# Attention written out without its loop, outputs accumulated in a PSUM bank, tables read in place

## The chip, the core and the metric

The kernel runs on one core of a Trainium2 chip. The core has engines that run side by side and meet through semaphores: PE (matrix products, written into PSUM), DVE and ACT (vector and scalar work), POOL (vector work on SBUF alone), and SP, which here only issues DMAs. The metric is the time of one execution on the device, in microseconds (us).

## The reference

A residual stream x of 8 batches x 512 tokens x 128 channels passes four layers, each with a layer norm ahead: attention, experts, a state-space mixer, experts again. The change lies in attention alone. Cut to what matters:

```python
scores = einsum('bhid,bhjd->bhij', q, k) * SCALE          # 16 heads of 64, n = 512
dist = clip(coords[:, None] - coords[None, :], -64, 64) + 64
scores = scores + einsum('bhid,ijd->bhij', q, rel_k_emb[dist])
threshold = top_k(scores, 32)[0][..., -1:]
attn = softmax(where(scores < threshold, -inf, scores))
res, v_curr = 0, v
for i in range(3):
    a_v = einsum('bhij,bhjd->bhid', attn, v_curr)
    if i == 0: a_v = a_v + einsum('bhij,ijd->bhid', attn, rel_v_emb[dist])
    v_curr = a_v
    res = res + sigmoid(alphas_raw)[i] * v_curr
x = x + res @ Wout.T + bout
```

All of it is float32.

## The kernel before

Attention works on pairs of heads: 8 pairs for each of 8 batches, 64 iterations (`ITS`). An iteration has four slots, T = 0 to 3, one for each tile of 128 queries. The five engines each run the same list of slots with their own `body`; each step of a slot works on a tile some slots back (`z.back(n)`), so that the stages of a tile are spread over eight slots: product with the relative keys (L592), scores (L577, L580, and L605, which adds the skewed relative part), ACT's copy of the scores (L753, two slots back), DVE's search for the 32 largest (L866 to L880, three back), POOL's mask (L934 to L949), ACT's exponential (L794, four back), DVE's reciprocal (L845, five back), POOL's scaling (L959), PE's transposes (L646, six back). The search is eight MAX8 and six MATCH_REPLACE8 a slot, four and three for each of two heads. DVE lies one slot ahead of POOL's mask.

Once an iteration come q, k and v of the next pair (L671, L656, L662), the three mixing steps of the pair before (L562, ACT's copy L722, the transposes L620, POOL's weighted sum into `res`, L914 and L919), and the output product. At T = 2 PE waits for POOL's sum and makes it (L630) in the bank `MISC`, which q, k, v and the transposes of the mixing also use. In the same slot DVE adds that bank into the stream (L851).

`run_iterations` sets the order: iterations -1 to 3 are written out, 4 to 61 are a hardware loop of 29 trips with two iterations (8 slots) each, and 62 to 66 are written out again. In the loop, waits and addresses that depend on the trip are worked out in registers (`known`, L369). The set-up builds two tables in SBUF, `table_j` (weights and biases of q, k, v by pair) and `table_o` (output weights, the alphas and the bias of v). SP copies a pair's part of each into `pair_j` (L482) and `pair_o` (L489) once an iteration, since an engine's operand inside the loop would otherwise move with the trip, and it copies the batch's normed input into `xt` (L483). The relative-key product is made for each head with 64 rows of contraction, into a bank of its own (`RL[h]`), and ACT copies both (L782).

Of the kernel before, what the change touches and what calls it, by code (L numbers as in the profile page):

```python
# [16 lines left out]
P = 128  # L17
# [166 lines left out]
def set_up(nc, sem, sb, ps, a, k, t, wr, r):  # L184
# [20 lines left out]
    with nc.Block() as block:  # L205
# [74 lines left out]
        def _(dve):  # L280
# [5 lines left out]
            for T in range(NT):  # L286
                nc.vector.memset(t.prob[T][:, :, 0:HALF], 0.0)
                nc.vector.memset(t.prob[T][:, :, HALF + N:PADDED], 0.0)
            dve.wait_ge(w_in, 16 * LOADS)
# [19 lines left out]
            nc.vector.tensor_scalar(t.relk[:, NEAR:2 * NEAR], ps[5][:, 1:P], relk0[:, 0:1], None, ALU.subtract)  # L309
# [3 lines left out]
            nc.vector.tensor_scalar(t.relk[:, 0:NEAR], ps[5][:, 1:P], rel_last[:, 0:1], None, ALU.subtract)  # L313
# [20 lines left out]
class Slots:  # L334


    def __init__(self, g, par, T):
        self.g, self.par, self.i, self.T = g, par, g * 2 + par, T

    def half(self, d):  # L340

        return self.g + (self.par + d) // 2
# [30 lines left out]
def run_iterations(eng, body):  # L373


    first, last = 4, ITS - 2
    for i in range(-1, first):
        for T in range(NT):
            body(Slots(i // 2, i % 2, T), i % 2)
    with eng.Fori(first // 2, last // 2) as g:  # L380
        for par in range(2):
            for T in range(NT):
                body(Slots(g, par, T), par)
    for i in range(last, ITS + 3):
        for T in range(NT):
            body(Slots(i // 2, i % 2, T), i % 2)


def attention(nc, sem, sb, ps, k, t):
# [35 lines left out]
    s.pj_in = [sem(f"att_pj_in{q}") for q in range(2)]  # L425
    s.po_in = [sem(f"att_po_in{q}") for q in range(2)]
# [8 lines left out]
    pj = two("pair_j", [P, J_COLS])  # L435
    po = two("pair_o", [P, O_COLS])
# [23 lines left out]
    SC, RL, PT, U, MISC = ps[0:2], ps[2:4], ps[4:6], ps[6], ps[7]  # L460
    HEADS = [slice(h * DH, (h + 1) * DH) for h in range(2)]

    def mixing(z, par):

        T, old, av = z.T, z.iteration(-3), z.iteration(-2)
        if T == 3 and av is not None:
            return av, 1, par
        if T < 2 and old is not None:
            return old, T + 2, 1 - par
        return None  # L470

    with nc.Block() as block:
        @block.sync
        def _(sp):
            def body(z, par):
                T, q = z.T, z.T % 2
                if T == 2 and (it := z.iteration(1)) is not None:
                    at_pair, at_batch = known(sp, (it % PAIRS) * J_COLS, (it // PAIRS) * N)
                    c0 = known(sp, it - 1)[0]
                    if not early(c0):  # L480
                        sp.wait_ge(s.v_kept, c0)
                    sp.dma_start(pj[1 - par][:, :], t.TJf[:, bass.ds(at_pair, J_COLS)]).then_inc(s.pj_in[1 - par], 16)  # L482
                    sp.dma_start(xt[1 - par][:, :], t.XNT[:, bass.ds(at_batch, N)]).then_inc(s.pj_in[1 - par], 16)  # L483
                if T == 3 and (it := z.iteration(-1)) is not None:
                    at_out, = known(sp, (it % PAIRS) * O_COLS)
                    c0 = known(sp, it - 1)[0]
# [57 lines left out]
        def _(pe):  # L544
# [5 lines left out]
            def body(z, par):  # L550
# [33 lines left out]
                if a:  # L584
# [25 lines left out]
                if m and m[1] < 3:  # L610
                    it, step, mpar = m
# [3 lines left out]
                    if T == 3 and old is not None:  # L615
                        pe.wait_ge(s.out_added, old + 1)
                    elif T == 3 and prev is not None:
# [33 lines left out]
                if T == 0 and cur is not None:  # L651
                    pe.wait_ge(s.pj_in[par], 32 * (z.half(0) + 1))
# [3 lines left out]
                    nc.tensor.matmul(MISC[:, :], pj[par][:, J_WK:J_WK + P], xt[par][:, :],  # L656
                                     start=True, stop=True).then_inc(s.k_made, 1)
                if T == 1 and prev is not None:
                    if cur is not None:
                        pe.wait_ge(s.k_kept, cur + 1)  # L660
                    for jt in range(NT):
                        last = nc.tensor.matmul(MISC[:, jt * P:(jt + 1) * P], xt[1 - par][:, jt * P:(jt + 1) * P],  # L662
                                                pj[1 - par][:, J_WV:J_WV + P], start=True, stop=True)
                    last.then_inc(s.v_made, 1)
                if T == 3 and nxt is not None:
                    pe.wait_ge(s.pj_in[1 - par], 32 * (z.half(1) + 1))
# [4 lines left out]
                    nc.tensor.matmul(MISC[:, :], pj[1 - par][:, J_WQ:J_WQ + P], xt[1 - par][:, :],  # L671
# [24 lines left out]
                if m and m[1] < 3:  # L696
                    it, step, mpar = m
# [6 lines left out]
        def _(act):  # L704
            def body(z, par):
# [4 lines left out]
                if m:  # L710
                    it, step, mpar = m
                    act.wait_ge(s.mixed, it * ORDER + step)
                    if step == 1:
                        act.wait_ge(s.po_in[mpar], 16 * (z.half(-2) + 1))
# [6 lines left out]
                    bias = {"bias": po[mpar][:, O_BV:O_BV + 1]} if step == 1 else {}  # L721
# [33 lines left out]
                if m and m[1] < 3:  # L755
                    it, step, mpar = m
# [1174 lines left out]
```

## Time and profile before

| | us |
|---|---|
| median of 3 runs | 3138.28 (3134.51 to 3139.64) |
| the profiled execution, its own time | 3144.04 |
| its span in the profile | 3142.3 |
| attention, first to last search step of DVE | 64 to 2421 |
| busy in the span: DVE / PE / POOL / ACT | 2719.1 / 2607.6 / 2163.7 / 2027.7 |

"Busy" is the time in which an engine has work in flight. A wait names what ended an idle time; "issue" means that the profile shows nothing that did. Idle time of an engine that does not set the pace costs nothing, so the first thing to find is the engine that has none.

### The profile page before, as it was taken

To read this page: it belongs to the slowest core of one execution; us is meant where nothing else is said; L and a number is where in the kernel's file an instruction comes from. 1 tells how busy PE (TensorE), PEld (TensorE's weight loads), DVE (VectorE), ACT (ScalarE), POOL (GpSimd) and SP (SyncE) were. 2 spreads that over 40 slices of the span, in tenths; PEclk is the share of its full clock that TensorE was granted. 3 is DMA by queue.
4 is the path that set the end of the run, shared out by engine and by line. 5 is a ranking of instruction groups with operands and counts; after the bars stand their busy time and mean duration, and the time that the engine had idled before them with its cause. 6 is when DMAs were issued, how large, how long until landed. Compare 5 with 4: busy or idle time off the path is not lost. (4 is left out here: it accounts for less than half of the span.)

```text
span 3142.3 us, 66621 instructions
## 1 busy us (share of the span) xinstructions
PE 2607.6 (83%) x15200; PEld 1498.6 (48%) x15200; DVE 2719.1 (87%) x6639; ACT 2027.7 (65%) x6207; POOL 2163.7 (69%) x2732
## 2 busy tenths in 40 slices
PE   4788888888788888888888888888888685988857
PEld 2444444444444444444444444444444444777743
DVE  5999999999999999999999999999998374765646
ACT  2677777877777777777777777777787152222214
POOL 1788888888888888888888888888888142221105
PEclk7899999999999999999999999999999696776659
DMA  4444444444444444444444444444443000000001
GB/s 119 118 132 134 129 127 125 129 132 125 131 126 129 127 127 127 128 126 130 131 129 126 130 125 134 125 125 131 127 131 100 4 29 14 8 6 1 0 8 48
DMA packets 401017, 318.44 MB, mean 101 GB/s; under 512 B 33246, under 2 KB 388648, under 8 KB 400808
## 3 DMA queue, kind: packets, MB, share of 16 engines
q1 hardware_dynamic: 398660, 314.18, 34.7%
q10 hardware_dynamic: 2148, 2.33, 0.3%
q14 instruction: 182, 1.49, 0.2%
q8 instruction: 27, 0.44, 0.1%
HBM read 139.48 MB, written 136.58 MB: 88 GB/s over the span
## 5 line engine op out<-in xcount | busy, mean ns | idle before, releaser
L870 DVE MAX8 top<-work 128x8 f32<-128x512 f32 x1536 | 980.7, 681 | 0.0
L880 DVE MATCH_REPLACE8 work<-top,work 128x512 f32<-128x512 f32 x1024 | 685.5, 678 | 0.0
L949 POOL TENSOR_TENSOR scores<-scores,cut 128x512 f32<-128x512 f32 x512 | 643.7, 1279 | 0.0
L562 PE MATMUL bank<-probs_t,u 128*64 128x512 f32 x2048 | 467.7, 598 | 1.4 <-ACT u L760 1.4
L794 ACT ACTIVATE probs_of_tile<-scores,minus_max_and_least 128x512 f32<-128x512 f32 x512 | 373.9, 748 | 89.7 <-POOL scores L949 89.2
L959 POOL TENSOR_SCALAR probs_of_tile<-probs_of_tile,inverse 128x512 f32<-128x512 f32 x512 | 349.0, 692 | 84.1 <-DVE inverse L845 61.4
L867 DVE MAX8 top<-scores 128x8 f32<-128x512 f32 x512 | 325.9, 679 | 82.8 <-issue 63.5
L940 POOL TENSOR_SCALAR cut<-scores,minus_max_and_least 128x512 f32<-128x512 f32 x512 | 354.2, 692 | 62.7 <-issue 39.5
L880 DVE MATCH_REPLACE8 work<-top,scores 128x512 f32<-128x512 f32 x512 | 342.7, 678 | 0.0
L771 ACT ACTIVATE probs_t<-bank 128x512 f32<-128x512 f32 x512 | 283.6, 609 | 66.7 <-PE bank L646 66.5
L945 POOL TENSOR_SCALAR cut<-cut 128x512 f32<-128x512 f32 x512 | 305.8, 613 | 21.5
L646 PE MATMUL bank<-identity,probs_of_tile 128*128 128x128 f32 x2048 | 310.9, 302 | 8.5 <-POOL probs_of_tile L959 8.5
L753 ACT ACTIVATE scores<-bank 128x512 f32<-128x512 f32 x512 | 273.5, 584 | 40.6 <-PE bank L605 40.6
L630 PE MATMUL bank<-pair_o,res 128*128 128x128 f32 x512 | 109.5, 382 | 228.7 <-POOL res L919 228.0
L646 PEld LDWEIGHTS bank<-identity,probs_of_tile 128*128 128x128 f32 x2048 | 268.0, 158 | 28.6 <-issue 19.1
L562 PE MATMUL bank<-probs_t,v 128*64 128x512 f32 x1024 | 257.3, 648 | 0.0
L562 PEld LDWEIGHTS bank<-probs_t,u 128*64 128x64 f32 x2048 | 135.7, 136 | 242.2 <-issue 240.4
L934 POOL TENSOR_SCALAR minus_max_and_least<-top 128x4 f32<-128x4 f32 x256 | 50.1, 196 | 238.5 <-issue 194.1
L630 PEld LDWEIGHTS bank<-pair_o,res 128*128 128x128 f32 x512 | 94.3, 276 | 249.4 <-issue 232.3
L731 ACT ACTIVATE band<-band 128x129 f32<-128x129 f32 x512 | 154.3, 303 | 61.6 <-DMA band<-probs_scratch 61.0
L577 PE MATMUL bank<-keys_left,qt 64*128 64x64 f32 (+3 forms) x1024 | 186.1, 441 | 1.8 <-ACT scores L753 1.5
L1634 POOL TENSOR_TENSOR mixer_a_spread<-rest_after,mixer_a 128x1024 f32<-128x1024 f32 x32 | 66.8, 2090 | 174.5 <-PE bank L1491 143.2
(251 smaller groups left out, 5062.7 us busy)
## 6 DMA issues: line engine op xcount, KB each, us to landing
probs_scratch<-probs_of_tile SPq DMA_DIRECT2D x256, 256.0 KB, 2.5
band<-probs_scratch SPq DMA_DIRECT2D x256, 256.0 KB, 3.2
rel_scratch<-rel SPq DMA_DIRECT2D x256, 254.0 KB, 3.1
relj<-rel_scratch SPq DMA_DIRECT2D x256, 128.0 KB, 2.3
relj<-rel_scratch SPq DMA_DIRECT2D x512, 64.0 KB, 2.5
xt<-stream_normed_t SPq DMA_DIRECT2D x64, 256.0 KB, 2.4
pair_j<-table_j SPq DMA_DIRECT2D x64, 193.5 KB, 2.2
pair_o<-table_o SPq DMA_DIRECT2D x64, 66.0 KB, 1.9
```

Of the source, the lines that this page charges most:

```text
L562: last = nc.tensor.matmul(U[HEADS[h], :], lhs, pt[mpar][:, h, jt, :], start=(jt == 0), stop=(jt == NT - 1 and step > 0))
L646: last = nc.tensor.transpose(PT[h][:, jt * P:(jt + 1) * P], t.prob[Td][:, h, HALF + jt * P:HALF + (jt + 1) * P], k.ident[:, :])
L753: nc.scalar.activation(sc[Tb][:, h, :], SC[h][:, :], ACT.Copy).then_inc(s.scores_kept, 1)
L771: nc.scalar.activation(pt[dpar][:, h, :, Td * P:(Td + 1) * P], PT[h][:, :].rearrange("p (j i) -> p j i", j=NT), ACT.Copy).then_inc(s.probs ...
L794: nc.scalar.activation(t.prob[Tx][:, h, HALF:HALF + N], sc[Tx][:, h, :], ACT.Exp, bias=neg[q][:, h, 0:1], accum_out=rs[Tx][:, h:h + 1]).th ...
L867: nc.vector.max(top[q][:, h, 0:8], sc[Tc][:, h, :]).then_inc(s.tops, 1)
L870: nc.vector.max(top[q][:, h, 8 * r:8 * r + 8], work[:, h, :]).then_inc(s.next_tops, 1)
L880: nc.vector.match_replace(out=work[:, h, :], in_to_replace=top[q][:, h, 8 * r:8 * r + 8], in_values=sc[Tc][:, h, :] if r == 0 else work[:, ...
L940: nc.gpsimd.tensor_scalar(cut[:, h, :], sc[Tc][:, h, :], neg[q][:, h, 1:2], STEEP, ALU.add, ALU.mult).then_inc(s.compared, 1)
L945: nc.gpsimd.tensor_scalar(cut[:, h, :], cut[:, h, :], 0.0, NEG, ALU.min, ALU.max).then_inc(s.cut, 1)
L949: nc.gpsimd.tensor_tensor(sc[Tc][:, h, :], sc[Tc][:, h, :], cut[:, h, :], ALU.add).then_inc(s.masked, 1)
L959: nc.gpsimd.tensor_scalar(row, row, inv[Ty][:, h:h + 1], 1.0, ALU.mult, ALU.mult).then_inc(s.probs, 1)
```

## The change

- The loop is gone: all 64 iterations, and the slots around them, are written out on every engine. Waits and addresses are constants.
- Output products of the 8 pairs of a batch accumulate in a bank `OUT`. DVE adds it into the stream once a batch, after the last pair. PE waits for that addition only at a batch's first pair.
- `pair_j` and `pair_o` and their DMAs are gone; the engines read `table_j` and `table_o` in place, at an offset known for each iteration. `xt` is still copied.
- The relative keys are kept as a table of 128 rows x 2 x 254 with zeros where a head's column block meets the other head's rows. One matmul of 128 rows and 508 columns into one bank takes the place of two, and one ACT copy of 508 takes the place of two of 254. This frees the bank for `OUT`.

```diff
-    first, last = 4, ITS - 2
-    for i in range(-1, first):
-        for T in range(NT):
-            body(Slots(i // 2, i % 2, T), i % 2)
-    with eng.Fori(first // 2, last // 2) as g:
-        for par in range(2):
+    for T in range(NT):
+        body(Slots(-1, PAIRS - 1, T), 1)
+
+    def batch(g, count=PAIRS):
+        for c in range(count):
             for T in range(NT):
-                body(Slots(g, par, T), par)
-    for i in range(last, ITS + 3):
-        for T in range(NT):
-            body(Slots(i // 2, i % 2, T), i % 2)
+                body(Slots(g, c, T), c % 2)
+
+    for g in range(B):
+        batch(g)
+    batch(B, 3)
...
-    SC, RL, PT, U, MISC = ps[0:2], ps[2:4], ps[4:6], ps[6], ps[7]
+    SC, RL, OUT, PT, U, MISC = ps[0:2], ps[2], ps[3], ps[4:6], ps[6], ps[7]
...
-                    sp.dma_start(pj[1 - par][:, :], t.TJf[:, bass.ds(at_pair, J_COLS)]).then_inc(s.pj_in[1 - par], 16)
-                    sp.dma_start(xt[1 - par][:, :], t.XNT[:, bass.ds(at_batch, N)]).then_inc(s.pj_in[1 - par], 16)
-                if T == 3 and (it := z.iteration(-1)) is not None:
-                    at_out, = known(sp, (it % PAIRS) * O_COLS)
-                    c0 = known(sp, it - 1)[0]
-                    if not early(c0):
-                        sp.wait_ge(s.out_made, c0)
-                    sp.dma_start(po[1 - par][:, :], t.TOf[:, bass.ds(at_out, O_COLS)]).then_inc(s.po_in[1 - par], 16)
+                    sp.dma_start(xt[1 - par][:, :], t.XNT[:, bass.ds(at_batch, N)]).then_inc(s.xt_in[1 - par], 16)
...
-                    for h in range(2):
-                        last = nc.tensor.matmul(RL[h][:, 0:2 * NEAR], qt[par][HEADS[h], Ta * P:(Ta + 1) * P],
-                                                t.relk[HEADS[h], :], start=True, stop=True)
-                    last.then_inc(s.rel_made, 1)
+                    nc.tensor.matmul(RL[:, 0:4 * NEAR], qt[par][:, Ta * P:(Ta + 1) * P],
+                                     t.relk[:, :, :].rearrange("p h c -> p (h c)"),
+                                     start=True, stop=True).then_inc(s.rel_made, 1)
...
                 if T == 2 and old is not None:
                     pe.wait_ge(s.res_chain, old * 5 + 5)
-                    pe.wait_ge(s.po_in[1 - par], 16 * (z.half(-3) + 1))
-                    if prev is not None:
-                        pe.wait_ge(s.v_kept, prev + 1)
+                    pair = z.pair(-3)
+                    if pair == 0 and not early(batches := batch_of(z)):
+                        pe.wait_ge(s.out_added, batches)
                     for jt in range(NT):
-                        last = nc.tensor.matmul(MISC[:, jt * P:(jt + 1) * P], res[:, jt * P:(jt + 1) * P],
-                                                po[1 - par][:, O_W:O_W + P], start=True, stop=True)
+                        last = nc.tensor.matmul(OUT[:, jt * P:(jt + 1) * P], res[:, jt * P:(jt + 1) * P],
+                                                t.TO[:, pair, O_W:O_W + P], start=(pair == 0 and jt == 0),
+                                                stop=(pair == PAIRS - 1 and jt == NT - 1))
...
-                    for h in range(2):
-                        last = nc.scalar.activation(rel[sp2][:, h, :], RL[h][:, 0:2 * NEAR], ACT.Copy)
-                    last.then_inc(s.rel_kept, 1)
+                    nc.scalar.activation(rel[sp2][:, :, :].rearrange("p h c -> p (h c)"), RL[:, 0:4 * NEAR],
+                                         ACT.Copy).then_inc(s.rel_kept, 1)
...
-                    if old is not None and T == 2:
+                    if old is not None and T == 2 and z.pair(-3) == PAIRS - 1:
                         dve.wait_ge(s.out_made, old + 1)
-                        if not early(old):
-                            dve.wait_ge(s.out_added, old)
-                        Xb = k.X[:, bass.ds((old // PAIRS) * N, N)]
-                        nc.vector.tensor_tensor(Xb, MISC[:, :], Xb, ALU.add).then_inc(s.out_added, 1)
+                        Xb = k.X[:, bass.ds((z.g - 1) * N, N)]
+                        nc.vector.tensor_tensor(Xb, OUT[:, :], Xb, ALU.add).then_inc(s.out_added, 1)
```

DVE at the end of a loop trip before: `work` is the copy of the scores that the search shortens, L380 is the loop.

```order
L870 MAX top<-work 128x8
L880 MATCH_REPLACE work<-top,work 128x512 x2
L369 REGISTER_ALU
L870 MAX top<-work 128x8
L369 REGISTER_ALU
L870 MAX top<-work 128x8
L380 REGISTER_ALU
L380 COMPARE_AND_BRANCH
```

The same engine after, in an iteration whose pair is not the last of its batch, from the reciprocal of T = 2 to that of T = 3.

```order
L845 RECIPROCAL inverse<-row_sums 128x2
L868 MAX top<-work 128x8 x2
L878 MATCH_REPLACE work<-top,work 128x512 x2
L868 MAX top<-work 128x8 x2
L865 MAX top<-scores 128x8 x2
L878 MATCH_REPLACE work<-top,scores 128x512 x2
L868 MAX top<-work 128x8 x2
L878 MATCH_REPLACE work<-top,work 128x512 x2
L845 RECIPROCAL inverse<-row_sums 128x2
```

The branch and the register instructions are gone, and no addition follows the reciprocal at T = 2.

PE in the slot T = 2 before, inside the loop, from the scores to the output product.

```order
L577 MATMUL bank<-keys_left,qt 128x64 x2
L580 MATMUL bank<-keys_right,qt 128x448 x2
L369 REGISTER_ALU
L592 MATMUL bank<-rel_keys,qt 128x254 x2
L369 ISA
L605 MATMUL bank<-relj,identity 64x192 x4
L625 ISA
L626 REGISTER_ALU
L630 MATMUL bank<-pair_o,res 128x128 x4
```

The same place after.

```order
L582 MATMUL bank<-keys_left,qt 128x64 x2
L585 MATMUL bank<-keys_right,qt 128x448 x2
L596 MATMUL bank<-rel_keys,qt 128x508
L609 MATMUL bank<-relj,identity 64x192 x4
L632 MATMUL bank<-table_o,res 128x128 x4
```

The order of the products is the same; the pair of 254 columns is one of 508, and the output product reads the table itself.

## Rows read from the trace of the kernel before

**Rows 1.** The page: busy us (share of the span) xinstructions of each engine.

```profile
PE 2607.6 (83%) x15200; PEld 1498.6 (48%) x15200; DVE 2719.1 (87%) x6639; ACT 2027.7 (65%) x6207; POOL 2163.7 (69%) x2732
```

**Rows 2.** DVE's groups, 200 to 2400 us: busy us, mean ns | idle before, releaser.

```profile
L870 DVE MAX8 top<-work 128x8 f32<-128x512 f32 x1431 | 913.8, 681 | 0.0
...
L867 DVE MAX8 top<-scores 128x8 f32<-128x512 f32 x476 | 303.0, 679 | 71.9 <-issue 63.5 <-ACT scores L753 8.5
```

**Rows 3.** Waits of DVE, 200 to 2400 us: us in total, times, longest.

```profile
DVE top L867 <- issue: 63.5, 25, 3.3
DVE top L867 <- ACT scores L753: 8.5, 3, 2.9
```

**Rows 4.** Timeline of DVE: start us, us, instruction, xcount [idle before <-releaser].

```profile
64.43 1.29 DVE L867 MAX8 top<-scores 128x8 f32<-128x512 f32 x2 [10.90 <-ACT scores L753]
...
253.30 1.29 DVE L867 MAX8 top<-scores 128x8 f32<-128x512 f32 x2 [2.96 <-issue]
...
993.27 1.29 DVE L867 MAX8 top<-scores 128x8 f32<-128x512 f32 x2 [2.63 <-issue]
...
1067.52 1.29 DVE L867 MAX8 top<-scores 128x8 f32<-128x512 f32 x2 [2.79 <-ACT scores L753]
...
1076.30 1.27 DVE L867 MAX8 top<-scores 128x8 f32<-128x512 f32 x2
...
1085.07 1.27 DVE L867 MAX8 top<-scores 128x8 f32<-128x512 f32 x2
...
1090.15 0.67 DVE L851 TENSOR_TENSOR stream<-bank,stream 128x512 f32 x1
1090.73 1.28 DVE L870 MAX8 top<-work 128x8 f32<-128x512 f32 x2
...
2420.99 0.14 DVE L845 RECIPROCAL inverse<-row_sums 128x2 f32<-128x2 f32 x1
```

**Rows 5.** Busy time by stretch, one ahead of the loop's first return, one at its end.

```profile
64.00:250.00 186.00, 148.58 (x896) 78.83 (x898) 185.57 (x442) 132.93 (x408) 145.00 (x194) 0.88 0.45 128
2260.00:2400.00 140.00, 119.84 (x770) 65.51 (x764) 140.00 (x335) 109.13 (x342) 120.63 (x162) 0.95 0.45 129
```

Columns: stretch, its us, busy us (xinstructions) of PE, PEld, DVE, ACT, POOL, the clock granted to PE, the DMA share, GB/s.

**Rows 6.** POOL: a wait from 200 to 2400 us, and its timeline at T = 2.

```profile
POOL minus_max_and_least L934 <- issue: 178.0, 120, 2.1
...
1056.10 0.20 POOL L934 TENSOR_SCALAR minus_max_and_least<-top 128x4 f32<-128x4 f32 x1 [1.79 <-issue]
```

**Rows 7.** PE: timeline, then its longest wait from 200 to 2400 us.

```profile
51.41 2.08 PE L671 MATMUL bank<-xt,pair_j 128*128 128x512 f32 x2 [4.02 <-DMA xt<-stream_normed_t]
...
1047.53 1.13 PE L630 MATMUL bank<-pair_o,res 128*128 128x128 f32 x8 [3.15 <-POOL res L919]
...
1067.85 1.12 PE L656 MATMUL bank<-xt,pair_j 128*128 128x512 f32 x2 [0.33 <-ACT u L760]
1068.81 0.38 PE L684 MATMUL bank<-identity,band 128*128 128x128 f32 x2
...
1078.29 0.59 PE L592 MATMUL bank<-rel_keys,qt 64*128 64x254 f32 x4
1078.82 0.56 PE L605 MATMUL bank<-relj,identity 64*64 64x192 f32 x8
1085.82 2.04 PE L630 MATMUL bank<-pair_o,res 128*128 128x128 f32 x8 [6.45 <-POOL res L919]
...
PE bank L630 <- POOL res L919: 216.7, 58, 6.6
```

**Rows 8.** Timeline of SP's queue.

```profile
1047.81 0.56 SPq L482 DMA_DIRECT2D pair_j<-table_j  x1
1048.50 0.55 SPq L483 DMA_DIRECT2D xt<-stream_normed_t  x1
```

**Rows 9.** Instruction queue, 60 to 250 us, then 250 to 2250: packets, MB, share.

```profile
q14 instruction: 17, 0.14, 0.2%
...
q14 instruction: 136, 1.11, 0.2%
```

More of the change, by code:

```diff
@@ L288, in _ @@
                 nc.vector.memset(t.prob[T][:, :, HALF + N:PADDED], 0.0)
+            for s in range(2):
+                nc.vector.memset(t.relk[(1 - s) * DH:(2 - s) * DH, s, :], 0.0)
             dve.wait_ge(w_in, 16 * LOADS)
@@ L308, in _ @@
                                     relv0_col[:, 0:1], None, ALU.add)
-            nc.vector.tensor_scalar(t.relk[:, NEAR:2 * NEAR], ps[5][:, 1:P], relk0[:, 0:1], None, ALU.subtract)
+            for s in range(2):
+                half = slice(s * DH, (s + 1) * DH)
+                nc.vector.tensor_scalar(t.relk[half, s, NEAR:2 * NEAR], ps[5][half, 1:P], relk0[half, 0:1], None,
+                                        ALU.subtract)
             nc.vector.tensor_scalar(column(t.TJ[:, :, J_BKR:J_BKR + 1]), ps[4][:, PAIRS:2 * PAIRS],
@@ L312, in _ @@
             dve.wait_ge(chain, 4)
-            nc.vector.tensor_scalar(t.relk[:, 0:NEAR], ps[5][:, 1:P], rel_last[:, 0:1], None, ALU.subtract)
+            for s in range(2):
+                half = slice(s * DH, (s + 1) * DH)
+                nc.vector.tensor_scalar(t.relk[half, s, 0:NEAR], ps[5][half, 1:P], rel_last[half, 0:1], None,
+                                        ALU.subtract)
             nc.vector.tensor_scalar(column(t.TJ[:, :, J_BKL:J_BKL + 1]), ps[4][:, PAIRS:2 * PAIRS],
@@ L424, in attention @@
     s.bias_added = sem("att_bias_added")
-    s.pj_in = [sem(f"att_pj_in{q}") for q in range(2)]
-    s.po_in = [sem(f"att_po_in{q}") for q in range(2)]
+    s.xt_in = [sem(f"att_xt_in{q}") for q in range(2)]
     s.rel_stored = [sem(f"att_rel_stored{q}") for q in range(2)]
@@ L466, in mixing @@
         if T == 3 and av is not None:
-            return av, 1, par
+            return av, 1, par, z.pair(-2)
         if T < 2 and old is not None:
-            return old, T + 2, 1 - par
+            return old, T + 2, 1 - par, z.pair(-3)
         return None
@@ L655, in body @@
                         pe.wait_ge(s.u_kept, m[0] * 2 + 2)
-                    nc.tensor.matmul(MISC[:, :], pj[par][:, J_WK:J_WK + P], xt[par][:, :],
+                    nc.tensor.matmul(MISC[:, :], t.TJ[:, z.pair(0), J_WK:J_WK + P], xt[par][:, :],
                                      start=True, stop=True).then_inc(s.k_made, 1)
@@ L670, in body @@
                         pe.wait_ge(s.v_kept, prev + 1)
-                    nc.tensor.matmul(MISC[:, :], pj[1 - par][:, J_WQ:J_WQ + P], xt[1 - par][:, :],
+                    nc.tensor.matmul(MISC[:, :], t.TJ[:, z.pair(1), J_WQ:J_WQ + P], xt[1 - par][:, :],
                                      start=True, stop=True).then_inc(s.q_made, 1)
@@ L710, in body @@
                 if m:
-                    it, step, mpar = m
+                    it, step, mpar, pair = m
                     act.wait_ge(s.mixed, it * ORDER + step)
-                    if step == 1:
-                        act.wait_ge(s.po_in[mpar], 16 * (z.half(-2) + 1))
                     summed, turned = {1: (it * 5 - 3, it * 2), 2: (it * 5 - 1, it * 2 + 1),
@@ L720, in body @@
                         act.wait_ge(s.mixed_turned, turned)
-                    bias = {"bias": po[mpar][:, O_BV:O_BV + 1]} if step == 1 else {}
+                    bias = {"bias": t.TO[:, pair, O_BV:O_BV + 1]} if step == 1 else {}
                     nc.scalar.activation(mixed[(mpar + step - 1) % 2][:, :], U[:, :],
@@ L902, in body @@
                 if m:
[L903 to L904 removed]
+                    it, step, mpar, pair = m
+                    alpha = t.TO[:, pair, O_AL + step - 1:O_AL + step]
                     made, before = known(pool, it * ORDER + step, it * 5 + 2 * step - 3)
```

39 lines of the change are left out of this document (18 added, 21 removed).

## The prediction, made before the changed kernel ran

> **What bounds the kernel now.** I read the views in this order. First the page's busy times: DVE is the busiest engine [rows 1]. A share of the whole span proves little, because the last 700 us are other stages, so the attention stage is taken alone. There the DVE groups are almost nothing but the top-32 search: MAX8, 679 to 681 ns each [rows 2], and the replacements between them. The reader should look at the idle column: it is zero for every DVE group but one, the first MAX8 of a slot (L867), with 71.9 us. The waits of DVE say the same: 25 waits with nothing that the profile shows ("issue") and 3 put down to ACT, none longer than 3.3 us [rows 3]. The start of the stage, 10.9 us for ACT's first scores, is outside this window [rows 4].
>
> The timeline shows where they are. A slot starts every 8.77 us (1076.30, 1085.07) unless it is the first of a loop trip, where DVE idles 2.6 us on average, at most 3.3 [rows 3]: 993.27 and 1067.52 are such starts, one trip (8 slots) apart [rows 4]. The loop has 29 trips, so 28 returns; the 28 idles (25 + 3) are exactly these. Within a trip, and in the parts written out ahead of and behind the loop, DVE never idles: 185.57 busy of 186 us, and 140.00 of 140 [rows 5]. So the stage is paced by DVE, and what DVE loses apart from the search is the return of the loop and one addition into the stream per iteration (L851).
>
> **The change, part by part.** All times are of the profiled execution: span 3142.3, its own time 3144.04, which is 5.8 us above the median 3138.28. I take the savings from the profile off that median.
>
> 1. No loop: 63.5 + 8.5 = 72.0 us of DVE idle at its returns go [rows 3]. Nothing covers them now, as DVE is the pacemaker; each is worth its full length, if nothing else is late. POOL, ACT and PE also lose their returns, but these engines wait for DVE anyway. POOL waits 178.0 us before L934, whose input is DVE's last MAX8 of the slot, so that "issue" stands for DVE [rows 6].
>
> 2. One addition a batch in place of one an iteration: 64 become 8. One costs DVE 1090.73 - 1090.15 = 0.58 us from its start to the next one [rows 4]. The last three fall partly behind the search, so I count 54 removed while DVE paces: 54 x 0.58 = 31.3 us. The 7 that remain ahead of the end wait for the output matmul, which now ends 2.3 us before the addition (1085.82 + 2.04 against 1090.15 [rows 4, 7]).
>
> 3. The loop's register instructions, and a wait against a register before each search step, become constants. They hide behind 680 ns instructions: the written-out slots before the loop are no shorter (21 of them stand between 64.43 and 250.34, the end of the search before the idle at 253.30; less three additions that is 8.77 each [rows 4]). I count 0.
>
> 4. The relative-key product: two 64-row matmuls of 254 columns become one 128-row matmul of 508 columns with zeros in the other head's half. The pair now takes 0.53 us from start to start (1078.29 to 1078.82). A full 128-row matmul of 512 columns takes 1068.81 - 1067.85 = 0.96 us [rows 7]. That is 0.43 us more a slot, 1.72 an iteration, on PE alone. Bounds: 0 if a 508-column pass costs what the pair did, 2.08 - 0.53 = 1.55 us a slot at the lower clock, which a full matmul at the start of the stage shows [rows 7]. I take 0.43, since at full clock the row is nearly the same instruction. What covers it: PE goes from L630 at 1047.53 to the end of L605 at 1079.38 in 31.85 us, its short waits included, and then waits 6.45 us for POOL's sum [rows 7]. It becomes 31.85 + 1.72 = 33.57 us. DVE's iteration becomes 4 x 8.77 + 0.58 / 8 = 35.15 us. PE still arrives 1.6 us early. Were the cover gone, every 0.1 us of excess an iteration would cost 6.4 us in all.
>
> The Trainium skill ("TensorEngine Tiling (Array Packing)", Theoretical Speedup and Key Properties) speaks against this part: a contraction of 64 rows is worth up to a factor of 2 in row tiling, and a change of tiling mode drains the array. By the factor the new matmul would be 1.06 us, against 0.96 by the row, which leaves the sum as it is; a drain is priced by no row here.
>
> 5. ACT copies the product once with 508 elements, not twice with 254. That can only shorten its list, and ACT is busy 109 of 140 us [rows 5], so 0.
>
> 6. pair_j and pair_o are no longer copied. SP issues two DMAs fewer an iteration: pair_j takes 0.69 us of the queue before xt goes out (1047.81 to 1048.50 [rows 8]). The queue moves earlier and no wait of DVE hangs on it; 0 in the steady part. At the start of the stage it gives 0.69 us back, while the product costs up to 1.55 more there. Together I take +0.4 us.
>
> 7. MISC is free of the output and OUT holds it, so PE's transposes at T = 3 no longer wait for DVE's addition, nor the output matmul for the copy of v. What PE waits for before L630 is POOL's sum [rows 7], which stays: 0. The new wait, for the last batch's addition, has 35 us of room. The merged product has one bank: POOL and DVE never touch it, ACT frees it within the same slot as now. Set-up gains four small DVE instructions, some 0.2 us.
>
> Sum: -72.0 - 31.3 + 0.4 + 0.2 = -102.7 us. As a cross-check DVE's search now runs from 64.43 to 2420.99 [rows 4], 2356.6 us; 256 slots of 8.77 and 7 additions are 2249.3, which is 107.3 less. The gap of 4 is slots that are a hundredth longer than 8.77. I take 104. Predicted: 3138.3 - 104 = **3034 us**.
>
> What is late next: PE, 1.6 us an iteration behind DVE; then POOL, which now waits 1.79 us for DVE before the mask of T = 2 (1056.10 [rows 6]).
>
> **Rivals.**
>
> *PE becomes the bound.* Against it is the 1.6 us above, and that PE's clock should rather rise: L630 takes 2.04 us, as at the lower level (1.2 GHz), after a wait of 6.45 us, but 1.13 after one of 3.15 [rows 7], and the waits shrink to 1 or 2 us; the mean granted clock is 0.95 [rows 5]. For it: no row has a 128-row matmul of this width between two groups of 64-row ones, so what the change of shape costs there is open. If the product cost twice my estimate, 0.86 us more a slot, PE's iteration would be 31.85 + 3.44 = 35.29; with 0.3 us more for other waits, 35.6, or 0.45 x 64 = 29 us: 3063. At the low clock, 31.85 + 6.2 = 38.05 is above today's 74.25 / 2 = 37.1 [rows 4], so about 3138 + 61 = 3199; I give this far end almost nothing.
>
> *New code stalls the engines (slower).* Written out, every instruction is fetched once. The instruction queue q14 brought 17 packets of 8 KB in the 190 us from 60 to 250 where most code is new, against 136 in 2000 us of the loop [rows 9]. At that rate 2250 us take about 200. If a quarter were DVE's and each stalled it as a return of the loop does (72.0 / 28 = 2.57 us), 50 x 2.57 = 129 us would eat the 104: 3163. It decides from 40 stalls on. Against it: DVE idled 0.43 us in the 186 us in which those 17 came, and nothing at the written-out end, 2325 to 2400 [rows 5]. The Trainium skill ("Runtime: NRT & Kernel Launch", Instruction fetch mechanics) has a straight run across a block mostly hidden and a jump outside the loaded blocks stalled; the two stretches agree for their short length, and none here is as long as the whole stage.
>
> *The idles at the loop's start stay.* If they came from something that recurs every 8 slots and not from the return, only 31 us would go: 3107. Against it: slots before 253 have none though 21 stand in a row.
>
> **How the numbers follow.** My forecast 0.84 (3026 to 3044: single terms off by some us). PE as the bound 0.07 (3044 to 3070 mostly). Code stalls 0.06, half of them partial (10 to 60 us lost), half beyond 40 stalls. Idles stay 0.03. The range 3024 to 3066 leaves out the far parts. The two of 3107 and 3163 lie outside. About 0.2% (6 us) is what a measurement can tell from no change: faster 0.95, within 0.02, slower 0.03.
>
> **What would show it.** In the changed profile: no "issue" idle before the first MAX8; 8 additions in place of 64; the product row near 1.1 us for its matmul; PE's wait for POOL's sum shrunk from 3.7 us (216.7 in 58 [rows 7]) to 1 or 2; last MAX8 near 2316. Wrong, if DVE shows waits for ACT's scores (PE is the bound), if DVE idles at places spread through the slots (code), or if slots are longer than 8.78 us.

## The result, and the profile after

| kernel | median us (lowest to highest, runs) | iteration, us |
|---|---|---|
| before, same chip | 3138.96 (3134.51 to 3143.19, 4) | 36.90 |
| changed | 3255.37 (3252.03 to 3264.05, 4) | 38.90 |

The changed kernel is slower: 1.0375 times the time before, 95% interval 1.0349 to 1.0402, about 117 us. The forecast was 3034. "Iteration" is the distance between the first and the last start of PE's product for v, divided by 63; before, the loop's returns and the additions are in it.

The page of the changed kernel, busy us and share of each engine ([rows 1] before):

```profile
PE 2768.9 (85%) x14688; PEld 1443.0 (44%) x14688; DVE 2706.1 (83%) x6587; ACT 2008.0 (62%) x5951; POOL 2167.8 (66%) x2732
```

PE has 512 instructions fewer and is busy 161 us longer. Two searches mark the stage: DVE's first MAX8 of a slot ran from 64.4 to 2412.2 before and runs from 66.4 to 2534.4 now, so the stage takes 120.2 us more, which is what the span gained (3142.3 to 3262.3). The rest of the kernel is as it was.

The same mark in DVE's groups, from 200 to 2500 us (busy us, mean ns | idle before, releasers), and the additions. [rows 2] answer to them.

```profile
L865 DVE MAX8 top<-scores 128x8 f32<-128x512 f32 x473 | 303.8, 684 | 200.5 <-ACT scores L754 179.2 <-POOL minus_max_and_least L932 21.0
...
L849 DVE TENSOR_TENSOR stream<-bank,stream 128x512 f32<-128x512 f32 x7 | 4.8, 692 | 0.4
```

The loop's "issue" idles are gone [rows 3], and so are all but one addition a batch. But DVE now idles 200.5 us in 2300, 3.4 us an iteration, 179.2 of them for ACT's copy of the scores. It no longer sets the pace. The waits of PE and ACT, first in the changed kernel from 200 to 2500 us (us in total, times, longest), lead to what does:

```profile
PE bank L687 <- ACT probs_t L772: 217.7, 70, 4.7
...
ACT mixed L723 <- PE bank L696: 261.0, 59, 5.4
ACT band L732 <- DMA band<-probs_scratch: 132.7, 84, 3.1
```

and in the kernel before from 200 to 2400 us:

```profile
PE bank L684 <- ACT probs_t L771: 33.9, 49, 3.2
...
ACT band L731 <- DMA band<-probs_scratch: 56.2, 51, 2.2
```

PE's wait for POOL's sum, 216.7 us before [rows 7], is gone altogether, where the forecast left 1 or 2 us of it an iteration. A wait of the same size stands elsewhere: PE in front of its transposes of the band waits for ACT, ACT waits for PE, and ACT waits for a DMA. When engines wait for each other like this, no engine's busy time limits the pace, but a **ring**: a chain that leaves an engine and returns to it one iteration later. It can be followed. The timeline of the changed kernel, starting where PE has ended the mixing of slot T = 0 and begins T = 1:

```profile
1048.24 1.02 PE L582 MATMUL bank<-keys_left,qt 64*128 64x448 f32 x4
...
1048.36 0.60 ACT L723 ACTIVATE mixed<-bank 128x512 f32<-128x512 f32 x1 [0.81 <-PE bank L567]
...
1052.95 0.63 ACT L782 ACTIVATE rel<-bank 128x508 f32<-128x508 f32 x1
...
1053.61 0.54 SPq L513 DMA_DIRECT2D rel_scratch<-rel  x1
...
1054.24 0.56 SPq L523 DMA_DIRECT2D band<-probs_scratch  x1
...
1058.45 0.31 ACT L732 ACTIVATE band<-band 128x129 f32<-128x129 f32 x1 [2.71 <-DMA band<-probs_scratch]
...
1061.42 1.08 ACT L772 ACTIVATE probs_t<-bank 128x512 f32<-128x512 f32 x2
...
1062.16 0.66 PE L687 MATMUL bank<-identity,band 128*128 128x128 f32 x2 [4.33 <-ACT probs_t L772]
...
1062.75 4.92 PE L567 MATMUL bank<-probs_t,v 128*64 128x512 f32 x16
...
1068.45 0.60 PE L582 MATMUL bank<-keys_left,qt 64*128 64x192 f32 x4
...
1087.23 1.02 PE L582 MATMUL bank<-keys_left,qt 64*128 64x448 f32 x4
```

Read it down. ACT starts its slot when PE's mixing is done, works through its list, and copies the relative part late (L782). SP can store that copy only then (L513), and SP's load of the band (L523) stands behind the store in the same queue, though it needs nothing of it. ACT's next slot needs that band first (L732); only behind it come the copies `probs_t`, for which PE waits before the band's transposes, and behind those on PE stands the long mixing step L567. Two more slots of PE, T = 3 and T = 0, and the ring closes at 1087.23. The same points before:

```profile
1037.70 1.02 PE L577 MATMUL bank<-keys_left,qt 64*128 64x448 f32 x4
...
1042.15 0.67 ACT L782 ACTIVATE rel<-bank 128x254 f32<-128x254 f32 x2
...
1043.48 0.56 SPq L518 DMA_DIRECT2D band<-probs_scratch  x1
...
1046.68 0.31 ACT L731 ACTIVATE band<-band 128x129 f32<-128x129 f32 x1 [1.27 <-DMA band<-probs_scratch]
...
1050.30 0.44 PE L684 MATMUL bank<-identity,band 128*128 128x128 f32 x2 [0.77 <-ACT probs_t L771]
...
1050.66 3.65 PE L562 MATMUL bank<-probs_t,v 128*64 128x512 f32 x16
...
1055.11 0.59 PE L577 MATMUL bank<-keys_left,qt 64*128 64x192 f32 x4
...
1072.70 1.02 PE L577 MATMUL bank<-keys_left,qt 64*128 64x448 f32 x4
```

| link of the ring, us | before | after |
|---|---|---|
| PE ends T = 0, to ACT's relative copy done | 5.12 | 5.34 |
| to ACT reading the band | 3.86 | 4.87 |
| to PE's transposes of the band | 3.62 | 3.71 |
| to PE starting T = 3 (the mixing with v) | 4.81 | 6.29 |
| PE's slots T = 3 and T = 0 | 17.59 | 18.78 |
| one turn | 35.00 | 38.99 |

Before, one turn took 35.0 us and DVE's own iteration 4 x 8.77 + 0.58 = 35.7 [rows 4], plus the loop's return. The ring was there, 0.7 us short of being seen. After, it takes 39.0, DVE's own iteration 35.15, and the measured one is 38.90. Of the 4.0 us more in this turn, 1.2 are the merged product in two slots, 1.5 the mixing, 1.0 the band's DMA.

The last two shares are those of this turn, not of the stage. In the 46 turns of the changed kernel between 300 and 2100 us that the trace shows, the median from the issue of the band's DMA to ACT's use is 3.2 us; in the 28 of 49 turns before in which ACT waited for it, the median is 3.2 us too. The median from the band's transposes to T = 3 is 6.48 us (6.14 at least), against 4.81 in the turn shown before. So in the typical turn the DMA takes no longer than before, and the mixing costs 1.7 us rather than 1.5.

What the mixing lost is the clock. Granted clock in windows of the changed kernel (columns as in [rows 5]), the first half of the mixing step and its second half:

```profile
1062.75:1065.35 2.60, 2.60 (x7) 0.76 (x8) 2.60 (x7) 1.91 (x6) 2.52 (x4) 0.50 0.42 110
1065.35:1067.50 2.15, 2.15 (x13) 0.70 (x10) 2.15 (x6) 0.00 (x0) 2.05 (x3) 1.00 0.40 114
```

It begins at 1.2 GHz, right behind a wait of 4.33 us. Before, PE waited almost as long in that slot, 3.15 + 0.77 us, but the longer wait lay ahead of L630 and the transposes, and the mixing took 3.65. Where it was 6.45 us [rows 7], L630 ran at the low clock, 2.04 us of it, and the mixing that followed was back at 3.65:

```profile
1085.82:1087.80 1.98, 1.98 (x9) 1.98 (x10) 1.98 (x6) 0.84 (x2) 1.73 (x3) 0.50 0.71 248
...
1090.09 3.65 PE L562 MATMUL bank<-probs_t,v 128*64 128x512 f32 x16
```

That it is so in most iterations is seen in the groups of PE, 200 to 2200 us (busy us, mean ns of one matmul | idle), before and then after:

```profile
L562 PE MATMUL bank<-probs_t,v 128*64 128x512 f32 x868 | 216.5, 643 | 0.0
```

```profile
L567 PE MATMUL bank<-probs_t,v 128*64 128x512 f32 x832 | 285.4, 850 | 0.0
```

The mean clock from 200 to 2200 us is 0.94 in both kernels. The slow time has moved with the wait: a matmul of the output product takes 383 ns before (L630) and 288 ns after (L632). So removing PE's wait for POOL did not remove waiting; it moved it to where it costs.

### The profile page after: what moved, and what is told of

It reads as the page before. It is cut to its first block and busy times, and to the rows that moved or that the text cites. A ratio compares the mean times of both kernels' runs of the same rounds, so it can differ in the third digit from the quotient of the medians.

```text
span 3262.3 us, 57866 instructions
## 1 busy us (share of the span) xinstructions
PE 2768.9 (85%) x14688; PEld 1443.0 (44%) x14688; DVE 2706.1 (83%) x6587; ACT 2008.0 (62%) x5951; POOL 2167.8 (66%) x2732
## 5 line engine op out<-in xcount | busy, mean ns | idle before, releaser
L567 PE MATMUL bank<-probs_t,u 128*64 128x512 f32 x2048 | 469.4, 601 | 1.4 <-ACT u L761 1.4
L567 PE MATMUL bank<-probs_t,v 128*64 128x512 f32 x1024 | 352.7, 853 | 0.0
L687 PE MATMUL bank<-identity,band 128*128 128x128 f32 x512 | 113.2, 307 | 239.5 <-ACT probs_t L772 238.7
L596 PE MATMUL bank<-rel_keys,qt 128*128 128x508 f32 x512 | 290.8, 650 | 5.9 <-issue 4.8
L649 PE MATMUL bank<-identity,probs_of_tile 128*128 128x128 f32 x2048 | 270.6, 275 | 7.1 <-POOL probs_of_tile L957 6.1
L567 PEld LDWEIGHTS bank<-probs_t,u 128*64 128x64 f32 x2048 | 136.1, 137 | 243.4 <-issue 241.6
L649 PEld LDWEIGHTS bank<-identity,probs_of_tile 128*128 128x128 f32 x2048 | 229.6, 141 | 27.5 <-issue 20.2
L732 ACT ACTIVATE band<-band 128x129 f32<-128x129 f32 x512 | 154.3, 303 | 137.4 <-DMA band<-probs_scratch 136.3
L723 ACT ACTIVATE mixed<-bank,table_o 128x512 f32<-128x512 f32 x64 | 44.0, 687 | 284.8 <-PE bank L696 284.8
L687 PEld LDWEIGHTS bank<-identity,band 128*128 128x128 f32 x512 | 65.7, 152 | 323.3 <-issue 316.4
```

Source lines behind the costliest of these rows:

```text
L567: last = nc.tensor.matmul(U[HEADS[h], :], lhs, pt[mpar][:, h, jt, :], start=(jt == 0), stop=(jt == NT - 1 and step > 0))
L596: nc.tensor.matmul(RL[:, 0:4 * NEAR], qt[par][:, Ta * P:(Ta + 1) * P], t.relk[:, :, :].rearrange("p h c -> p (h c)"), start=True, stop=Tru ...
L649: last = nc.tensor.transpose(PT[h][:, jt * P:(jt + 1) * P], t.prob[Td][:, h, HALF + jt * P:HALF + (jt + 1) * P], k.ident[:, :])
```

## The experiments

Each starts from one of the two kernels. Times are medians with the ratio to the kernel before on the same chip (95% interval) and the iteration as above. In the first group of runs that kernel stood at 3134.34, in the second at 3134.38, in the third at 3136.11.

| kernel | us | ratio | iteration |
|---|---|---|---|
| e1 written out only | 3091.74 | 0.9852 (0.9792 to 0.9912) | 36.35 |
| e2 merged product in the loop | 3234.83 | 1.0308 (1.0231 to 1.0385) | 38.59 |
| e3 half the product | 3138.12 | 1.0024 (0.9993 to 1.0056) | 36.97 |
| e5 mixing ahead of the band | 3097.15 | 0.9869 (0.9817 to 0.9921) | 36.29 |
| e4 band's load first | 3028.01 | 0.9662 (0.9622 to 0.9701) | 35.20 |
| e6 both moves | 3025.70 | 0.9658 (0.9623 to 0.9692) | 35.20 |
| e7 written out, both moves | 3062.46 | 0.9772 (0.9718 to 0.9825) | 35.71 |
| e8 PE kept busy | 3107.76 | 0.9916 (0.9880 to 0.9952) | 36.59 |
| e9 loop, merged, band first | 3130.50 | 0.9982 (0.9955 to 1.0010) | 36.81 |
| e10 loop, band first | 3124.60 | 0.9963 (0.9944 to 0.9981) | 36.74 |

### Which part of the change costs: e1 and e2

e1 is the changed kernel with the two 64-row products, their two banks, and the output product in `MISC` with an addition each iteration, as before. What is left of the change is the written-out order and the tables in place.

```diff
-                    nc.tensor.matmul(RL[:, 0:4 * NEAR], qt[par][:, Ta * P:(Ta + 1) * P],
-                                     t.relk[:, :, :].rearrange("p h c -> p (h c)"),
-                                     start=True, stop=True).then_inc(s.rel_made, 1)
+                    for h in range(2):
+                        last = nc.tensor.matmul(RL[h][:, 0:2 * NEAR], qt[par][HEADS[h], Ta * P:(Ta + 1) * P],
+                                                t.relk[HEADS[h], h, :], start=True, stop=True)
+                    last.then_inc(s.rel_made, 1)
```

> Written out and with the tables read in place, as the changed kernel, but with the relative-key product as two 64-row matmuls into two banks, and the output product in MISC with DVE's addition in every iteration, as before. Ring theory (a chain PE, ACT, SP's band load, ACT, PE closes once an iteration; 35.0 us long in the kernel before, 39.0 in the changed one, and the merged product lengthened it): the ring stays at 35.0, just under DVE's 35.7, so 3139 - 72 = 3067, up to 3090 if the ring closes now and then. Code theory (written-out code slows some engine): it stays slow, 3255 + 31 for the additions, some 3285. Theory that the OUT bank and its waits are at fault: 3067 as well, since they are absent here.

e2 is the kernel before, loop and all, with the merged product alone: the table of 2 x 254 columns, one matmul, one copy.

> The kernel before, loop and all, with the one 128-row product of 508 columns and the one ACT copy in place of the two. Ring theory: the ring grows by about 0.5 us in each of two slots and by what the lower clock adds after PE's longer wait, to 38 or 39 us an iteration, against 37.1 with the loop: 3139 + 64 x 1 to 2 = 3200 to 3270, and DVE shows waits for ACT's scores. PE-throughput theory (only PE's total work counts, 33.6 us an iteration): no change, 3139. Code theory: no change, 3139. OUT-bank theory: no change, 3139.

e1 is 43 us faster than before and e2 100 us slower. The loss is the merged product's: it makes the loop kernel slow as well, whose code is fetched as before and which has no bank `OUT`. DVE's waits in e2, 200 to 2400 us:

```profile
DVE top L873 <- ACT scores L760: 104.8, 121, 2.6
DVE top L873 <- issue: 26.6, 12, 2.4
```

The wait for the scores has displaced the loop's idles. But e1 missed its number by some 25 us: the ring costs something there too. DVE waits 20.4 us for ACT's scores from 200 to 2200 us. PE in e1 at T = 2:

```profile
1038.31 0.41 PE L689 MATMUL bank<-identity,band 128*128 128x128 f32 x2 [3.21 <-ACT probs_t L774]
1038.65 5.35 PE L567 MATMUL bank<-probs_t,v 128*64 128x512 f32 x16
```

The mixing is partly at the low clock here too, 1.7 us longer. It is not so in every turn: behind a wait of 3.06 us it took 3.65 us at 1146.59 and 5.35 at 1216.12, and in 15 of 50 turns from 300 to 2100 us the way from the band's transposes to T = 3 is 4.78 us, as short as at full clock. A turn of 35.0 at full clock is below e1's DVE iteration of 35.7, one of 36.7 is above it, and 36.35 was measured. A ring so near may fall on either side: a turn with the low clock is late, and a late turn makes PE wait in front of the mixing. That the one keeps up the other is argued from these rows; e8 below tests the half of it that is the clock.

### Columns or shape: e3

In the changed kernel, the 128-row product has 254 columns instead of 508, and its result serves both heads; what it leaves out is the second head's own relative scores.

```diff
-                    nc.tensor.matmul(RL[:, 0:4 * NEAR], qt[par][:, Ta * P:(Ta + 1) * P],
-                                     t.relk[:, :, :].rearrange("p h c -> p (h c)"),
-                                     start=True, stop=True).then_inc(s.rel_made, 1)
+                    nc.tensor.matmul(RL[:, 0:2 * NEAR], qt[par][:, Ta * P:(Ta + 1) * P],
+                                     t.relk[:, 0, :], start=True, stop=True).then_inc(s.rel_made, 1)
```

> The changed kernel with a 128-row product of only 254 columns; ACT copies these columns for both heads in two steps. Left out: the relative scores of the second head of each pair are those of the first. PE's product takes 0.53 us instead of 1.0 and ACT's copies what they took before; all else is the changed kernel. Ring theory: the ring is back at about 35.0 us and DVE at 35.15 sets the pace or nearly so: 3034 to 3065. Code theory and OUT-bank theory: 3255 stays, less at most 0.5 us x 4 x 64 = 128 if PE alone were the bound, which is 3127.

It gives back the 117 us and no more, some 70 us short of what was expected. PE's timeline in e3, from the scores through the product to the relative part:

```profile
1022.02 0.70 PE L585 MATMUL bank<-keys_right,qt 64*128 64x320 f32 x4
1022.66 0.70 PE L596 MATMUL bank<-rel_keys,qt 128*128 128x254 f32 x2
1023.29 0.66 PE L608 MATMUL bank<-relj,identity 64*64 64x256 f32 x8
```

And the changed kernel in the same slot:

```profile
1068.88 0.71 PE L585 MATMUL bank<-keys_right,qt 64*128 64x320 f32 x4
1069.52 1.12 PE L596 MATMUL bank<-rel_keys,qt 128*128 128x508 f32 x2
1070.57 0.66 PE L609 MATMUL bank<-relj,identity 64*64 64x256 f32 x8
```

From L585 to the relative part it is 1.69 us after, 1.27 in e3, and 1.06 before (L580 at 1055.54, L605 at 1056.60). The 254 further columns cost 0.42, as forecast; another 0.21 us is the 128-row shape between two groups of 64 rows. Half of it stands at each side: from L585 to the product it is 0.64 us in e3 against 0.54 before (L580 to L592, 1056.08), and from the product to the relative part 0.63 against 0.52. The rule of the Trainium skill that was weighed in part 4 ("TensorEngine Tiling (Array Packing)", Key Properties), that a change of tiling mode drains the array, fits this; 0.21 us is then its price here for both changes, but no run separates a drain from another cost of the shape. e3 keeps that and, in most turns, the low clock in the mixing (5.35 us at 1015.46, behind a wait of 3.57), so DVE still waits 74.0 us for scores from 200 to 2200 us.

### Is it the ring: e4, e5 and e6

In e5 PE does the mixing with v ahead of the band's transposes, which alone need the late band:

```diff
+                if T == 2 and av is not None:
+                    pe.wait_ge(s.probs_kept, (av + 1) * 2 * NT)
+                    pe.wait_ge(s.v_kept, av + 1)
+                    mix(av, par, 0)
+
                 e = z.back(7)
...
                 if T == 2 and av is not None:
-                    pe.wait_ge(s.probs_kept, (av + 1) * 2 * NT)
-                    pe.wait_ge(s.v_kept, av + 1)
-                    mix(av, par, 0)
                     pe.wait_ge(s.band_kept, (av + 1) * NT)
```

> The changed kernel with one thing moved on PE at T = 2: the eight products of the first mixing step stand ahead of the transposes of the band, so PE does them while ACT copies the scaled rows, and only the two products with the relative values wait for the band. Same instructions. Ring theory: the chain loses the 3.6 us of these products and the low clock behind PE's 4.3 us wait, so it is 36 us or less; DVE sets the pace or nearly: 3034 to 3075. PE-throughput, code and OUT-bank theories: no change, 3255.

In e4 nothing changes but the order of two blocks of SP: the store of the relative part goes behind the band's load.

```diff
-                if a:
-                    it, Ta, n = a
-                    c0, c1 = known(sp, n + 1, 48 * (it * 2 + Ta // 2))
-                    sp.wait_ge(s.rel_kept, c0)
...
-                    sp.dma_start(bass.AP(t.r_dram[q], P, [[2 * ROW, P], [ROW, 2], [1, 2 * NEAR]]),
-                                 rel[q][:, :, :]).then_inc(s.rel_stored[q], 16)
-
                 if d:
...
+                if a:
+                    it, Ta, n = a
+                    c0, c1 = known(sp, n + 1, 48 * (it * 2 + Ta // 2))
+                    sp.wait_ge(s.rel_kept, c0)
...
+                    sp.dma_start(bass.AP(t.r_dram[q], P, [[2 * ROW, P], [ROW, 2], [1, 2 * NEAR]]),
+                                 rel[q][:, :, :]).then_inc(s.rel_stored[q], 16)
```

> The changed kernel with one thing moved on SP: in each slot the load of the band stands ahead of the store of the relative products, so that it no longer waits for ACT's copy of them. Same DMAs. Ring theory: at T = 2 ACT waits 2.7 us for the band in the changed kernel, and this wait is a link of the ring; without most of it the iteration falls from 39.0 by 2 to 2.7 us: 3255 - 64 x 2 to 2.7 = 3082 to 3127. PE-throughput and OUT-bank theories: no change, 3255.

e6 has both.

> The changed kernel with both moves: the first mixing step ahead of the band's transposes on PE (alone 3097), and the band load ahead of the store on SP. Ring theory: the ring falls under DVE's 35.15 us in nearly all iterations, and the forecast of the prediction holds at last: 3034 to 3055. If the 3097 was left by something else than the ring (for instance PE's total work of 34.4 us and its low clock): 3080 to 3097.

All three keep every instruction of the changed kernel. e5 takes some 158 us off it, e4 227, e6 230. e4's queue and PE, from its timeline:

```profile
1002.29 0.37 SPq L514 DMA_DIRECT2D band<-probs_scratch  x1
...
1002.75 0.54 SPq L524 DMA_DIRECT2D rel_scratch<-rel  x1
...
1004.96 0.31 ACT L732 ACTIVATE band<-band 128x129 f32<-128x129 f32 x1 [0.36 <-DMA band<-probs_scratch]
...
1006.29 1.16 PE L632 MATMUL bank<-table_o,res 128*128 128x128 f32 x8 [1.54 <-POOL res L917]
...
1008.72 0.41 PE L687 MATMUL bank<-identity,band 128*128 128x128 f32 x2 [0.40 <-ACT probs_t L772]
1009.06 3.65 PE L567 MATMUL bank<-probs_t,v 128*64 128x512 f32 x16
```

The load goes out 0.46 us ahead of the store and no longer waits for ACT's last copy. From its issue to ACT's first use it is 2.67 us, against 4.21 in the changed kernel. This is the tightest turn of e4, the only one of 52 between 300 and 2100 us in which ACT still waited for this band. In the median turn the gain is the earlier issue: the load goes out 3.7 us after PE has ended T = 0, against 6.0 in the changed kernel. The median landing of all band loads also falls, from 3.3 us to 2.7. PE waits 0.40 us in front of the mixing, which is back at 3.65. And the stage as a whole, e4 from 300 to 2300 us:

```profile
300.00:2300.00 2000.00, 1864.50 (x10930) 891.14 (x10926) 2000.00 (x4787) 1604.22 (x4839) 1762.54 (x2335) 1.00 0.42 128
```

DVE is busy 2000.00 of 2000 us with the merged product in place, and PE's clock is full. PE's work was never too much. e4 came out 54 us below the 3082 to 3127 that were expected from ACT's wait alone: with the wait in front of it, the slow clock in the mixing went too. e5 alone leaves ACT's late band, and PE then waits for it one step later, ahead of the band's own product; it landed some 20 us short of its number. PE in e5:

```profile
1036.79 3.65 PE L567 MATMUL bank<-probs_t,v 128*64 128x512 f32 x16
...
1042.51 1.08 PE L698 MATMUL bank<-band_t,rel_values 128*64 128x512 f32 x4 [1.70 <-ACT band_t L806]
```

With the load moved, moving the mixing too adds nothing that can be told (3028.01 and 3025.70). e6 is the fastest kernel here, e4 the same with one edit less, and both beat the kernel before by 3.4%.

### The additions and the loop: e7

e7 is e1 with both moves: the ring is open, and against e6 it has the 64-row products and an addition in every iteration.

> The kernel that is written out only, with two 64-row products and the output in MISC (3092 without moves), with both moves. Ring theory: DVE sets the pace at 35.7 us an iteration, 3139 - 72 = 3067. Against the two moves with the OUT bank, this prices the additions, 31 us.

DVE has no wait from 200 to 2200 us in e7 either. Its iteration is 35.71 and e6's 35.20: the additions are worth 0.51 us an iteration, 33 us in all (37 by the medians, whose intervals are wider). Against the iteration before, 36.90, the loop's end is worth 1.19 x 64 = 76 us.

### The clock alone: e8

In the changed kernel PE gets three products more, whose results nothing reads, right where it waits:

```diff
+                if T == 2 and av is not None:
+                    pe.wait_ge(s.probs_kept, (av + 1) * 2 * NT)
+                    if not early(av * ORDER):
+                        pe.wait_ge(s.mixed_kept, av * ORDER)
+                    for _ in range(3):
+                        nc.tensor.matmul(U[:, :], k.ident[:, :], pt[par][:, 0, 0, :], start=True, stop=True)
```

> The changed kernel with work added: ahead of the band's transposes at T = 2, where PE waits 4.3 us for ACT, it makes three products of 128x512 into U that nobody reads (2.9 us at full clock), so that its clock need not fall. If the low clock behind that wait is a part of the ring (4.92 us for the first mixing step in place of 3.65, and 0.2 to 0.3 in the transposes): 3255 - 64 x 1.3 to 1.5 = 3160 to 3172, though there is more work. If the clock plays no part: 3255 or a little more.

More work on PE made the changed kernel some 145 us faster. PE's timeline in e8:

```profile
1005.49 2.74 PE L682 MATMUL bank<-probs_t,identity 128*128 128x512 f32 x6
1008.84 0.41 PE L694 MATMUL bank<-identity,band 128*128 128x128 f32 x2 [0.61 <-ACT probs_t L779]
1009.18 3.66 PE L567 MATMUL bank<-probs_t,v 128*64 128x512 f32 x16
```

The mixing is 3.66 us again. On the turn shown above that saves 1.3 us, but that turn is one of the milder ones, and so the expectation was short. Over 200 to 2200 us a mixing step took 5.49 us in the changed kernel (285.4 us in 52 steps, L567 above) and takes 3.65 in e8 (201.0 in 55). That is 1.84 us a turn, 118 of the 145 us. The other 27 or so were not taken apart.

### Does the merged product cost anything with the ring open: e9 and e10

e10 is the kernel before with the band's load first, e9 is that with the merged product.

> The kernel before with only the band load moved. Ring theory: DVE sets the pace in the kernel before, the ring is just under it, so the move gains nothing: 3130 to 3139. If the ring already cost something before (the three waits for ACT's scores at the loop's returns), up to 9 us less.

> The kernel before with its loop, with the merged product (alone 3235) and the band load ahead of the store. Ring theory: the merged product costs nothing once the ring has room, so DVE sets the pace again: 3134 to 3145, and its waits are the loop's returns only. If the merged product costs by itself (PE's total work, 34.3 us of 37.1 an iteration): 3200 or more.

DVE's waits in e9, 200 to 2400 us:

```profile
DVE top L873 <- issue: 66.7, 28, 3.0
```

No wait for scores. The merged product costs 100 us in the loop kernel (e2), and about 6 with the ring open (e9 against e10, by intervals that overlap, so that it may be nothing). The kernel before loses little to the ring: e10 gains 11 us, 0.2% to 0.6% by its interval.

## Why the prediction was wrong

**The step that failed** is in part 4: "What covers it". It took PE's work from L630 to the end of L605, 31.85 us, and the wait of 6.45 us behind it, and read that wait as room. It was not room. In the slot shown before, PE's 3.15 us wait for POOL was followed by 0.77 us for ACT, so a PE that came earlier there waited for `probs_t`, and ACT for a band that hung on the mixing of the turn before. The wait of 6.45 us itself stands in an iteration that the loop's return had lengthened, and PE waited for no ACT behind it; that room went with the return. What was left was DVE's iteration less one turn of the ring: 35.7 less 35.0. Part 1 takes the return away, part 2 makes 35.7 into 35.15, and the product alone puts 1.2 in. The forecast had "PE still arrives 1.6 us early"; the ring arrives 3.8 us late. The same misreading is in part 7, where PE's wait for POOL's sum was held to be what PE waits for.

**Of the right kind but too small** was the product: 0.43 us forecast, 0.63 measured (1.69 less 1.06). The missing 0.21 is the shape, which the prediction had named as open.

**The clock** did not rise. "PE's clock should rather rise" rested on the waits shrinking; they moved in front of the mixing instead. The mean stayed at 0.94 from 200 to 2200 us, but the mixing, which is on the ring, took 4.92 us in the turn shown in place of 3.65. With the ring open the clock did rise as forecast: 1.00 in e4.

**The rival "PE becomes the bound"** had the right sign of mechanism: DVE waits for ACT's scores, as it said it would. It priced it by PE's total as well, 3063 us, and gave the far end, "about 3199", almost nothing. The measured 3255 is beyond even that, though the product ran at 1.12 us and not at the 2.08 of the low clock: a turn of the ring also holds ACT's list, the DMA and the slowed mixing. The price that was missing is that of a turn.

**What held**, as seen when the ring is open:

- Part 1: the loop's idles, 72.0 us forecast; 76 by the iteration of e7.
- Part 2: the additions, 31.3 us forecast; 33.
- The slot of 8.77 us and the iteration of 35.15; 35.20 in e4 and e6.
- The sum, 3034 us (its cross-check is 2249.2 and 107.4 by its own terms, a tenth off; nothing hangs on it); 3028.01 in e4 and 3025.70 in e6, with DVE busy all of 2000 us.
- PE's wait for POOL's sum "1 or 2" us: 1.54 in e4's turn.
- Parts 5 and 6 at nothing: e4 and e6 leave no room for a cost. In the changed kernel the copy of 508 is on the ring, but takes 0.63 us where the pair took 0.67.

**The rival on new code** is refuted for the whole stage. The instruction queues from 250 to 2250 us (packets, MB, share), in the changed kernel and then in e4:

```profile
q8 instruction: 83, 1.36, 0.3%
q14 instruction: 141, 1.16, 0.2%
```

```profile
q8 instruction: 91, 1.49, 0.3%
q14 instruction: 157, 1.29, 0.2%
```

A second queue appears that had no packet in the loop, and e4 brings 248 packets in that stretch; DVE did not idle for one of them. The rule of the Trainium skill ("Runtime: NRT & Kernel Launch", Instruction fetch mechanics), a straight run mostly hidden, holds here for 2000 us of it. The idles that recur without the loop, the third rival, did not occur: no "issue" stands among DVE's waits after.

**What stays open.** The band's DMA took 1.0 us longer from issue to use in the turn shown after (3.20 to 4.21). In 6 of 46 turns of the changed kernel it took over 4 us, and before in none of the 28 in which ACT waited for it; what it meets in those was not tried. Its median landing over 200 to 2200 us rose only from 3.2 to 3.3. Of DVE's 38.90 us, 35.15 are the work that was forecast and 3.4 idle; the last 0.3 counts as busy (1826.27 of 2000 us, or 35.5 an iteration), for no reason that a run shows. Why the mixing is slowed behind one wait and not behind another just as long is open too, and so is the part of e8's gain that is not the mixing's.

## What to carry to other kernels

The idle time of an engine in front of one instruction is not its slack. Before counting work as covered, follow what else the engine waits for behind that wait, back through the in-order queues until the chain returns to its start one iteration later, and compare that turn with the pacemaker's iteration: the difference is the room. Here one load stood behind one store on a queue that only issues DMAs, and swapping them turned a change that cost 3.7% into one that gains 3.4%.

## What the hardware showed that was not expected

- One 128-row product of 254 columns between groups of 64-row products took 0.21 us longer, from the product ahead to the one behind, than the two 64-row products of 254 columns that it stood for (1.27 against 1.06).
- Behind a wait of 3.2 to 4.3 us directly in front of the mixing step its 16 matmuls took 4.92 to 5.35 us instead of 3.65 in the turns shown, at a granted clock of 0.50 in the first half (changed kernel); three useless products in that gap brought 3.66 back. Such a wait does not always do it: in e3 the step took 3.65 us at 496.55, behind a wait of 3.71, and 5.35 at 531.76, behind one of 3.74.
